# Expert layer on one core: eight blocks for the relu's output, two of four pairs rounded by ScalarE

## The chip, the cores and the metric

The kernel is one program on one core of a Trainium2 chip. Its five engines are written here as the profile writes them: PE (TensorE; PEld is its weight load), DVE (VectorE), ACT (ScalarE), POOL (GpSimd) and SP (SyncE, which issues DMAs here). Each engine works through its own list of instructions in order and is held up only by semaphores. The metric is the device time of one launch in microseconds; lower is better.

## The reference, cut to what matters

Two layers run one after the other. The change lies in the first, a mixture of experts over 16 x 256 tokens of width 256:

```python
h = h_norm * gamma[:, None, :] + beta[:, None, :]          # gamma, beta from small tables per batch
probs = softmax(h_flat @ router_w); gates, idx = top_k(probs, 2)
hid  = relu(einsum('nd,edf->nef', h_flat, exp_w1) + exp_b1)   # 8 experts, 256 -> 1024
eout = einsum('nef,efd->ned', hid, exp_w2) + exp_b2           # 1024 -> 256
y = einsum('ned,ne->nd', eout, combine); x = x + y
```

The second layer (conditioned attention with 16 heads, then a feed-forward of width 1024) reads x and is not touched. All is fp32.

## The kernel before

**Stages.** `condition_and_route` normalises and routes the tokens (up to about 170 us of the trace) and writes every token's row to DRAM, sorted by expert. Then its expert stage runs over 39 tiles (`TILES`) of 256 tokens, each with one expert. After it `transformer` runs, from about 698 us.

**Splitting.** A product of fp32 numbers is made of three products of numbers in fp32r, a shorter format: each operand is rounded (the tile with `hi` in its name) and the rest, operand minus `hi`, is the second tile (`lo`); `PASSES` takes hi x hi, hi x lo and lo x hi. So each of four things has to be split for every tile: the tokens (htokT, from the PSUM bank ps_t), four parts of w1, the relu's output (hidT, four pairs g = 0 to 3 of 128x512) and four parts of w2. Both weights of all experts are resident in SBUF.

**Work of one tile t.** PE: `up(t)`, 48 matmuls into the four banks ps_h, one bank for each pair; `turn_in(t+1)`, four transposes of the next tokens into ps_t; `down(t-1)`, 48 matmuls into ps_y, in four parts k that need hidT pair k and w2 part k. `up(t)` starts with the semaphores htokT_split and w1_split, `down(t-1)` with y_ready (the previous result has been taken out of ps_y), w2_split and the pair's hidT_even or hidT_odd.

Who splits what, in the order of each list, before the change:

- ACT (`body`, L434 on): relu of blocks 0 to 3, rounding of w1 parts 0 to 3 for tile t+1, `take_in(t+1)` (rounds the tokens out of ps_t), relu 4, relu 5, w2 part 0, relu 6, w2 part 1, relu 7, w2 parts 2 and 3.
- DVE (`body`, L753 on): the rests of w1 parts 0 to 3 (`lower_w1`, L736), the rest of the tokens (`lower_tokens`, L741), then `split_hidden` for pairs 0 to 3: a rounding copy of each (L726), and for pairs 0 and 2 also the rest (L232); last `take_out(t-1)` (L750: ps_y plus bias into SBUF, which raises y_ready).
- POOL (`body`): the rest of pair 1 (L232), of w2 parts 0 and 1 (L357), of pair 3, of w2 parts 2 and 3.
- SP: loads tokens two tiles ahead, stores the result, loads the bias row.

The relu's output goes to `hid`, which has `HID_SLOTS` = 4 blocks of 128x256 laid over the buffer columns. Pair g therefore shares its place with pair g+2, and `relu` waits at each even f until the pair that stands there has been split:

```python
wait_free(act, sem("hidT_odd" if g % 2 else "hidT_even"), 2 * t + g // 2, alone=True)
```

That is pair g-2 of the same tile for g = 2 and 3, and pair g+2 of the tile before for g = 0 and 1.

Tiles 2 to 33 run in a hardware loop of four tiles a round, the first and last ones in straight code, with the same lists.

Of the kernel before, what the change touches and what calls it, by code (L numbers as in the profile page):

```python
# [16 lines left out]
P = 128  # L17
# [94 lines left out]
def condition_and_route(nc, ctx, io, keep):  # L112
# [79 lines left out]
    y = h2  # L192
    hid = columns[:].rearrange("p i n -> p (i n)").rearrange("p (s m) -> p s m", s=HID_SLOTS)

# [22 lines left out]

    cond = cond_weights(nc, sb, w1[:, E - 1, :])

# [7 lines left out]

    def lower_pair(eng, t, g):

        rows = slice(2 * g, 2 * g + 2)  # L230
        slots = slice(2 * g % HID_SLOTS, 2 * g % HID_SLOTS + 2)
        return eng.tensor_tensor(hidT["lo"][:, rows, :], hid[:, slots, :], hidT["hi"][:, rows, :].bitcast(F32), ALU.subtract)  # L232

# [69 lines left out]
    def _(pool):  # L303
# [47 lines left out]
        def lower_hidden(t, g):  # L351
            wait_alone(pool, sem("hid_rounded"), 2 * t + g // 2 + 1)
            lower_pair(pool, t, g).then_inc(sem("hidT_odd"), 1)

# [19 lines left out]
    def _(act):  # L374
# [39 lines left out]

        def relu(t, e, f):
            if f % 2 == 0:
                g = f // 2
                wait_alone(act, sem("up_done"), F * t + f + 2)
                wait_free(act, sem("hidT_odd" if g % 2 else "hidT_even"), 2 * t + g // 2, alone=True)
            act.activation(hid[:, f % HID_SLOTS, :], ps_h[f // 2][:, (f % 2) * TOK:(f % 2 + 1) * TOK], ACT.Relu,  # L420
                           bias=b1[:, bass.ds(e, 1), f:f + 1].rearrange("p e f -> p (e f)")).then_inc(sem("hid_ready"), 1)

        def upper_w1(t, e, k):
# [10 lines left out]
        def body(tile):  # L434
            t = tile.t
            if a_tile(t):
                e = expert_of(t)
                for f in range(4):
                    relu(t, e, f)
            if a_tile(t + 1):  # L440
                ahead = expert_of(t + 1)
                for k in range(PARTS):
                    upper_w1(t + 1, ahead, k)
                take_in(t + 1)
            if a_tile(t):
                for f, pieces in ((4, ()), (5, (0,)), (6, (1,)), (7, (2, 3))):
                    relu(t, e, f)
                    for k in pieces:
                        upper_w2(t, e, k)

# [98 lines left out]
    def _(dve):  # L549
# [171 lines left out]
        def split_hidden(t, g):  # L721
            dve.wait_ge(sem("hid_ready"), F * t + 2 * (g + 1))
            wait_free(dve, sem("w2_used"), PARTS * (t - 1) + g + 1)
            rows = slice(2 * g, 2 * g + 2)
            slots = slice(2 * g % HID_SLOTS, 2 * g % HID_SLOTS + 2)
            rounded = dve.tensor_copy(hidT["hi"][:, rows, :], hid[:, slots, :])  # L726
            if g % 2:
                rounded.then_inc(sem("hid_rounded"), 1)
            else:
                rounded.then_inc(sem("hid_upper"), 1)  # L730
                dve.wait_ge(sem("hid_upper"), 2 * t + g // 2 + 1)
                lower_pair(dve, t, g).then_inc(sem("hidT_even"), 1)

# [19 lines left out]
        def body(tile):  # L753
            t = tile.t
            if a_tile(t + 1):
                e = dve.value_load(tile_tab[0:1, 0, bass.ds(t + 1, 1)], min_val=0, max_val=E - 1)
                for k in range(PARTS):
                    lower_w1(t + 1, e, k)
                lower_tokens(t + 1)
            if a_tile(t):  # L760
                for g in range(F // 2):
                    split_hidden(t, g)
            if a_tile(t - 1):
                take_out(tile.ahead(-1))
# [54 lines left out]

def cond_weights(nc, sb, room):  # L820

    def place(rows, start, width):
# [38 lines left out]
def cond_scalar(nc, act, w, vec, sem):  # L861
# [4 lines left out]
    act.wait_ge(sem("low_ready"), 1)  # L866
    act.activation(w["exp"][:], w["low"][:], ACT.Exp).then_inc(sem("soft_exp_ready"), 1)
    act.wait_ge(sem("soft_exp_ready"), 1)
    act.activation(w["log"][:], w["exp"][:], ACT.Ln, bias=1.0).then_inc(sem("soft_log_ready"), 1)
    act.wait_ge(sem("sine_ready"), 1)  # L870
# [3 lines left out]
def cond_vector(nc, dve, w, vec, ps_a, ps_b, gamma, beta, keep, sem):  # L874
# [912 lines left out]
```

## Time and profile before

| what | value |
|---|---|
| median of 3 runs (lowest, highest) | 1508.81 us (1507.02, 1511.48) |
| the profiled execution's own time | 1508.79 us |
| its span, first to last instruction | 1507.0 us |
| mean granted TensorE clock | 0.969 |
| busy over the span | PE 85%, DVE 66%, ACT 55%, POOL 42% |
| PE busy at 400 to 500 us | 94.67 us of 100 |

Busy time of PE counts each matmul to its modelled end, and successive matmuls overlap; how fast PE goes is read from the distance between the starts. Idle time in brackets names the engine whose signal ended it. The duration of a DVE or POOL instruction includes time in which it stood still after its start.

### The profile page before, as it was taken

What the parts mean: (1) busy time and instruction counts of PE and PEld (TensorE: products, weight loads), DVE (VectorE), ACT (ScalarE), POOL (GpSimd) and SP (SyncE); (2) the same over time, 40 slices, a digit from 0 to 9 for tenths busy, and PEclk for the clock granted to TensorE, in tenths of its full rate; (3) what the DMA queues carried; (4) which work ended last, traced back from release to release, by engine and by line L of the source; (5) the groups of instructions that cost most, each with busy time, mean ns of one, the idle gap of its engine ahead of it and who ended that gap; (6) DMA issues with size and microseconds to landing.
All of it is one profiled execution on the core that took longest, in us unless ns stands there. A gap on an engine that the chain in (4) does not pass through costs nothing. (4 is left out here: it accounts for less than half of the span.)

```text
span 1507.0 us, 35099 instructions
## 1 busy us (share of the span) xinstructions
PE 1286.2 (85%) x9859; PEld 1157.2 (77%) x9859; DVE 993.0 (66%) x2956; ACT 834.4 (55%) x2208; POOL 636.0 (42%) x595
## 2 busy tenths in 40 slices
PE   2666499999999999993589999999899999999996
PEld 2555399999999999993468878887788877797875
DVE  3887567667766766775557666666666765667552
ACT  2222266655656666561166666666666766666671
POOL 1677266666666666664213233323232232322211
PEclk9999999999999999997699999999999999999997
DMA  3676311111111111113666656556565666556520
GB/s 112 228 241 205 119 36 54 49 46 44 52 52 52 52 52 44 50 40 127 208 223 202 204 174 197 174 182 209 184 191 164 202 200 201 179 166 187 184 78 14
DMA packets 184810, 202.83 MB, mean 135 GB/s; under 512 B 18192, under 2 KB 172752, under 8 KB 184720
## 3 DMA queue, kind: packets, MB, share of 16 engines
q1 hardware_dynamic: 171920, 164.19, 34.8%
q10 hardware_dynamic: 6624, 20.84, 4.3%
q0 software_dynamic: 6176, 16.79, 3.3%
q8 instruction: 33, 0.54, 0.1%
q14 instruction: 57, 0.47, 0.1%
HBM read 155.89 MB, written 41.68 MB: 131 GB/s over the span
## 5 line engine op out<-in xcount | busy, mean ns | idle before, releaser
L1197 ACT ACTIVATE bias<-bias,neg_max 128x256 f32<-128x256 f32 x512 | 255.4, 501 | 207.3 <-DVE neg_max L1509 207.1
L420 ACT ACTIVATE columns<-ps_h,b_columns 128x256 f32<-128x256 f32 x312 | 134.6, 471 | 190.1 <-DVE hidT_lo L232 102.8
L357 POOL TENSOR_TENSOR w_lo<-w,w_hi 128x512 fp32r<-128x512 f32 x156 | 222.0, 1436 | 0.3
L1509 DVE CUSTOM_DVE_ANT_0 bias<-ps_s,bias 128x256 f32<-128x256 f32 x512 | 194.2, 416 | 31.5 <-PE ps_s L1285 14.9
L532 PE MATMUL ps_y<-w_hi,hidT_hi 128*128 128x256 f32 x624 | 181.3, 290 | 21.3 <-DVE token_rows L750 21.1
L519 PE MATMUL ps_h<-htokT_hi,w_hi 128*128 128x256 f32 x624 | 182.5, 293 | 11.0 <-DVE htokT_lo L741 10.4
L232 POOL TENSOR_TENSOR hidT_lo<-columns,hidT_hi 128x512 fp32r<-128x512 f32 x78 | 100.1, 1283 | 209.2 <-DVE hidT_hi L726 209.2
L736 DVE TENSOR_TENSOR w_lo<-w,w_hi 128x512 fp32r<-128x512 f32 x156 | 102.7, 715 | 119.7 <-ACT w_hi L425 119.7
L1283 PE MATMUL ps_s<-mask_f,minus_ident 128*128 128x256 f32 x512 | 155.4, 325 | 27.9 <-DVE neg_max L1509 15.4
L519 PE MATMUL ps_h<-htokT_hi,w_lo 128*128 128x256 f32 x624 | 178.5, 286 | 0.0
L519 PE MATMUL ps_h<-htokT_lo,w_hi 128*128 128x256 f32 x624 | 178.3, 286 | 0.0
L532 PE MATMUL ps_y<-w_lo,hidT_hi 128*128 128x256 f32 x624 | 177.3, 284 | 0.0
L532 PE MATMUL ps_y<-w_hi,hidT_lo 128*128 128x256 f32 x624 | 177.2, 284 | 0.0
L1297 PE MATMUL ps_p<-const,bias 128*128 128x128 f32 x1024 | 158.0, 277 | 14.5 <-ACT bias L1197 14.2
L1149 POOL TENSOR_TENSOR act_lo<-up_f,act_hi 128x512 fp32r<-128x512 f32 x64 | 82.6, 1291 | 208.2 <-ACT act_hi L1241 208.2
L726 DVE CAST hidT_hi<-columns 128x512 fp32r<-128x512 f32 x156 | 128.8, 825 | 31.6 <-ACT columns L420 29.7
L1283 PEld LDWEIGHTS ps_s<-mask_f,minus_ident 128*128 128x128 f32 x512 | 99.6, 195 | 60.5 <-DVE neg_max L1509 34.4
L532 PEld LDWEIGHTS ps_y<-w_hi,hidT_hi 128*128 128x128 f32 x624 | 120.2, 193 | 30.1 <-issue 22.6
L519 PEld LDWEIGHTS ps_h<-htokT_hi,w_hi 128*128 128x128 f32 x624 | 121.4, 195 | 18.8 <-issue 12.6
L1297 PEld LDWEIGHTS ps_p<-const,bias 128*128 128x128 f32 x1024 | 117.2, 142 | 24.0 <-issue 14.0
L1285 PE MATMUL ps_s<-k_stack,q_stack 128*128 128x256 f32 x512 | 135.3, 286 | 0.0
L1131 POOL TENSOR_TENSOR rstd<-mv,minus_half 128x2 f32<-128x2 f32 x32 | 23.1, 723 | 263.0 <-DVE mv L1568 175.2
(265 smaller groups left out, 3501.1 us busy)
## 6 DMA issues: line engine op xcount, KB each, us to landing
bias<-bias_dram SPq DMA_DIRECT2D x128, 512.0 KB, 3.8
w<-w_dram ACTq DMA_DIRECT2D x32, 512.0 KB, 4.7
xin<-dispatch SPq DMA_DIRECT2D x39, 256.0 KB, 2.7
expert_out<-token_rows SPq DMA_DIRECT2D x39, 256.0 KB, 2.2
q_stack<-q_hi_rows SPq DMA_DIRECT2D x64, 128.0 KB, 2.9
k_stack<-k_hi_rows SPq DMA_DIRECT2D x64, 128.0 KB, 2.8
q_stack<-q_lo_rows SPq DMA_DIRECT2D x64, 128.0 KB, 2.9
k_stack<-k_lo_rows SPq DMA_DIRECT2D x64, 128.0 KB, 2.9
```

Source lines behind the costliest of these rows:

```text
L232: return eng.tensor_tensor(hidT["lo"][:, rows, :], hid[:, slots, :], hidT["hi"][:, rows, :].bitcast(F32), ALU.subtract)
L357: pool.tensor_tensor(w2_part["lo"][:, k, :], w2_piece(e, k), w2_part["hi"][:, k, :].bitcast(F32), ALU.subtract).then_inc(sem("w2_split"), 1)
L420: act.activation(hid[:, f % HID_SLOTS, :], ps_h[f // 2][:, (f % 2) * TOK:(f % 2 + 1) * TOK], ACT.Relu, bias=b1[:, bass.ds(e, 1), f:f + 1]. ...
L519: last = pe.matmul(ps_h[f // 2][:, (f % 2) * TOK:(f % 2 + 1) * TOK], w1_part[a][:, C * (f // 4) + c, (f % 4) * P:(f % 4 + 1) * P], htokT[b ...
L532: last = pe.matmul(ps_y[j][:, 0:D], hidT[a][:, f, j * P:(j + 1) * P], w2_part[b][:, k, (f % 2) * D:(f % 2 + 1) * D], start=(f == 0 and n = ...
L726: rounded = dve.tensor_copy(hidT["hi"][:, rows, :], hid[:, slots, :])
L736: dve.tensor_tensor(w1_part["lo"][:, k, :], w1_piece(e, k), w1_part["hi"][:, k, :].bitcast(F32), ALU.subtract).then_inc(sem("w1_split"), 1)
L1197: act.activation(head_rows(h, j), head_rows(h, j), ACT.Exp, scale=-1.0, bias=neg_max[par][:, h, j:j + 1], accum_out=total[par][:, h, j:j + ...
L1283: pe.matmul(ps_s[h % 2][:, j * T:(j + 1) * T], minus_ident[:], mask_f[par][:, j, :], start=True, stop=False)
L1285: last = pe.matmul(ps_s[h % 2][:, j * T:(j + 1) * T], q_stack[par][:, h, j * P:(j + 1) * P].bitcast(F32R), k_stack[par][:, h // 2, :].bitc ...
L1297: last = pe.transpose(ps_p[h % 2][:, kt * T + j * P:kt * T + (j + 1) * P], head_rows(h, j)[:, kt * P:(kt + 1) * P], ident)
L1509: dve.tensor_tensor_reduce(head_rows(h, j), ps_s[h % 2][:, j * T:(j + 1) * T], head_rows(h, j), -1.0, LARGEST, ALU.add, ALU.min, neg_max[p ...
```

## The change

Three things change.

1. `hid` gets eight blocks: pairs 0 and 1 in the two halves of columns, pair 2 in the buffer xn (free in this stage), pair 3 in a new buffer hid_more. `relu` now waits only until the same pair of the tile before has been split.
2. Pairs 1 and 3 are rounded by ACT (`round_hidden`), no longer by DVE. The rests stay where they were: 0 and 2 on DVE, 1 and 3 on POOL.
3. The lists of ACT and DVE are put in another order: on both the tokens of the next tile come after w1 parts 0 and 1 instead of after all four, and on ACT all eight relus come before the tokens.

To make room for hid_more, five small tables of the conditioning (pre, neg, low, exp, log) are placed in the last expert's part of the w2 buffer, before that part is loaded.

```diff
-    hid = columns[:].rearrange("p i n -> p (i n)").rearrange("p (s m) -> p s m", s=HID_SLOTS)
+    hid = [columns[:, i, :].rearrange("p (s m) -> p s m", s=2) for i in range(2)] + [keep["xn"][:], sb("hid_more", [P, 2, TOK])[:]]
...
+            g = f // 2
             if f % 2 == 0:
-                g = f // 2
                 wait_alone(act, sem("up_done"), F * t + f + 2)
-                wait_free(act, sem("hidT_odd" if g % 2 else "hidT_even"), 2 * t + g // 2, alone=True)
+                wait_free(act, sem("hidT_odd" if g % 2 else "hidT_even"), 2 * (t - 1) + g // 2 + 1, alone=True)
...
+        def round_hidden(t, g):
+            act.wait_ge(sem("hid_ready"), F * t + 2 * (g + 1))
+            wait_free(act, sem("w2_used"), PARTS * (t - 1) + g + 1, alone=True)
+            act.activation(hidT["hi"][:, 2 * g:2 * g + 2, :], hid[g], ACT.Copy).then_inc(sem("hid_rounded"), 1)
...
             if a_tile(t + 1):
                 ahead = expert_of(t + 1)
-                for k in range(PARTS):
-                    upper_w1(t + 1, ahead, k)
+                upper_w1(t + 1, ahead, 0)
+                upper_w1(t + 1, ahead, 1)
+            if a_tile(t):
+                for f in range(4, F):
+                    relu(t, e, f)
+            if a_tile(t + 1):
                 take_in(t + 1)
+                upper_w1(t + 1, ahead, 2)
+                upper_w1(t + 1, ahead, 3)
             if a_tile(t):
-                for f, pieces in ((4, ()), (5, (0,)), (6, (1,)), (7, (2, 3))):
-                    relu(t, e, f)
-                    for k in pieces:
-                        upper_w2(t, e, k)
+                upper_w2(t, e, 0)
+                round_hidden(t, 1)
+                upper_w2(t, e, 1)
+                upper_w2(t, e, 2)
+                round_hidden(t, 3)
+                upper_w2(t, e, 3)
...
-            rounded = dve.tensor_copy(hidT["hi"][:, rows, :], hid[:, slots, :])
-            if g % 2:
-                rounded.then_inc(sem("hid_rounded"), 1)
-            else:
-                rounded.then_inc(sem("hid_upper"), 1)
-                dve.wait_ge(sem("hid_upper"), 2 * t + g // 2 + 1)
-                lower_pair(dve, t, g).then_inc(sem("hidT_even"), 1)
+            dve.tensor_copy(hidT["hi"][:, 2 * g:2 * g + 2, :], hid[g]).then_inc(sem("hid_upper"), 1)
+            dve.wait_ge(sem("hid_upper"), 2 * t + g // 2 + 1)
+            lower_pair(dve, g).then_inc(sem("hidT_even"), 1)
...
-                for k in range(PARTS):
-                    lower_w1(t + 1, e, k)
+                lower_w1(t + 1, e, 0)
+                lower_w1(t + 1, e, 1)
                 lower_tokens(t + 1)
+                lower_w1(t + 1, e, 2)
+                lower_w1(t + 1, e, 3)
             if a_tile(t):
-                for g in range(F // 2):
-                    split_hidden(t, g)
+                split_hidden(t, 0)
+                split_hidden(t, 2)
...
-        "pre": sb("pre", [P, C, B]), "neg": sb("neg", [P, C, B]), "low": sb("low", [P, C, B]),
-        "exp": sb("exp", [P, C, B]), "log": sb("log", [P, C, B]),
+        **{name: more[:, i * C * B:(i + 1) * C * B].rearrange("p (c b) -> p c b", c=C)
+           for i, name in enumerate(("pre", "neg", "low", "exp", "log"))},
```

DVE's list for the second tile, in the straight code ahead of the loop, before the change, from the tokens of the next tile on (columns is where the relu's blocks stand, token_rows the result):

```order
L736 TENSOR_TENSOR w_lo<-w,w_hi 128x512
L741 TENSOR_TENSOR htokT_lo<-ps_t,htokT_hi 128x512
L726 CAST hidT_hi<-columns 128x512
L232 TENSOR_TENSOR hidT_lo<-columns,hidT_hi 128x512
L726 CAST hidT_hi<-columns 128x512 x2
L232 TENSOR_TENSOR hidT_lo<-columns,hidT_hi 128x512
L726 CAST hidT_hi<-columns 128x512
L750 TENSOR_TENSOR token_rows<-ps_y,b_row 128x256 x2
```

And the same place in the changed kernel, from the rest of w1 part 1 on:

```order
L742 TENSOR_TENSOR w_lo<-w,w_hi 128x512
L747 TENSOR_TENSOR htokT_lo<-ps_t,htokT_hi 128x512
L742 ISA
L742 TENSOR_TENSOR w_lo<-w,w_hi 128x512
L742 ISA
L742 TENSOR_TENSOR w_lo<-w,w_hi 128x512
L736 CAST hidT_hi<-columns 128x512
L231 TENSOR_TENSOR hidT_lo<-columns,hidT_hi 128x512
L736 CAST hidT_hi<-xn 128x512
L231 TENSOR_TENSOR hidT_lo<-xn,hidT_hi 128x512
L756 TENSOR_TENSOR token_rows<-ps_y,b_row 128x256 x2
```

Two of four casts are gone between the tokens and the result, and two weight rests have moved behind the tokens.

ACT's list in the loop before the change, from the tokens to the second block of the third pair (ISA and REGISTER_ALU rows set up addresses and waits):

```order
L413 ACTIVATE htokT_hi<-ps_t 128x512 [waits up_done]
L68 REGISTER_ALU
L68 REGISTER_ALU [waits up_done]
L420 ISA [waits hidT_even]
L420 ACTIVATE columns<-ps_h,b_columns 128x256
L420 ISA
L420 ACTIVATE columns<-ps_h,b_columns 128x256
L68 ISA
L429 ISA [waits w2_used]
L429 ACTIVATE w_hi<-w 128x512
```

The changed kernel at the same place, from the tokens on:

```order
L412 ACTIVATE htokT_hi<-ps_t 128x512 [waits up_done]
L429 ISA [waits up_done]
L429 ACTIVATE w_hi<-w 128x512
L429 ISA [waits up_done]
L429 ACTIVATE w_hi<-w 128x512
L68 ISA
L433 ISA [waits w2_used]
L433 ACTIVATE w_hi<-w 128x512
L68 REGISTER_ALU [waits hid_ready]
L425 ACTIVATE hidT_hi<-columns 128x512 [waits w2_used]
```

The relus have left this place (they stand ahead of the tokens now), w1 parts 2 and 3 stand behind the tokens, and the rounding of pair 1 stands among the w2 parts, behind a wait for w2_used. PE's and POOL's lists are the same in both kernels.

## Rows read from the trace of the kernel before

**Rows 1.** Windows: stretch, its length, busy time per engine, granted clock, DMA.

```profile
400.00:500.00 100.00, 94.67 (x762) 91.42 (x761) 69.90 (x99) 60.75 (x129) 62.30 (x46) 1.00 0.17 52
```

**Rows 2.** Waits, 220 to 690 us: who for whom, total, times, longest.

```profile
POOL hidT_lo L232 <- DVE hidT_hi L726: 173.5, 72, 4.5
...
ACT columns L420 <- DVE hidT_lo L232: 94.9, 36, 2.8
...
PE ps_y L532 <- DVE token_rows L750: 20.7, 36, 3.7
...
PE ps_h L519 <- DVE htokT_lo L741: 6.5, 31, 0.2
```

**Rows 3.** Timeline of PE, one tile in the loop: start, us, what, idle before.

```profile
402.21 0.38 PE L532 MATMUL ps_y<-w_hi,hidT_hi 128*128 128x256 f32 x1 [0.48 <-DVE token_rows L750]
...
407.94 0.28 PE L532 MATMUL ps_y<-w_hi,hidT_lo 128*128 128x256 f32 x1
408.46 0.38 PE L519 MATMUL ps_h<-htokT_hi,w_hi 128*128 128x256 f32 x1 [0.24 <-DVE htokT_lo L741]
...
414.31 0.60 PE L507 MATMUL ps_t<-const,xin 128*128 128x128 f32 x4
415.40 0.38 PE L532 MATMUL ps_y<-w_hi,hidT_hi 128*128 128x256 f32 x1 [0.49 <-DVE token_rows L750]
```

**Rows 4.** Timeline of PE in the second and third tile.

```profile
192.24 0.60 PE L507 MATMUL ps_t<-const,xin 128*128 128x128 f32 x4
192.59 0.37 PE L532 MATMUL ps_y<-w_hi,hidT_hi 128*128 128x256 f32 x1
...
198.43 0.28 PE L519 MATMUL ps_h<-htokT_hi,w_hi 128*128 128x256 f32 x1
...
204.20 0.60 PE L507 MATMUL ps_t<-const,xin 128*128 128x128 f32 x4
```

**Rows 5.** Timeline of DVE, the same tile as rows 3.

```profile
404.98 2.63 DVE L736 TENSOR_TENSOR w_lo<-w,w_hi 128x512 fp32r<-128x512 f32 x4 [2.99 <-ACT w_hi L425]
407.53 0.68 DVE L741 TENSOR_TENSOR htokT_lo<-ps_t,htokT_hi 128x512 fp32r<-128x512 f32 x1
408.13 0.41 DVE L726 CAST hidT_hi<-columns 128x512 fp32r<-128x512 f32 x1
408.57 0.69 DVE L232 TENSOR_TENSOR hidT_lo<-columns,hidT_hi 128x512 fp32r<-128x512 f32 x1
...
411.37 1.67 DVE L232 TENSOR_TENSOR hidT_lo<-columns,hidT_hi 128x512 fp32r<-128x512 f32 x1
412.95 1.52 DVE L726 CAST hidT_hi<-columns 128x512 fp32r<-128x512 f32 x1
414.40 0.74 DVE L750 TENSOR_TENSOR token_rows<-ps_y,b_row 128x256 f32<-128x256 f32 x2
```

**Rows 6.** Timeline of POOL beside it, from two windows.

```profile
411.05 1.43 POOL L357 TENSOR_TENSOR w_lo<-w,w_hi 128x512 fp32r<-128x512 f32 x1
...
412.49 1.71 POOL L357 TENSOR_TENSOR w_lo<-w,w_hi 128x512 fp32r<-128x512 f32 x1
...
415.85 2.54 POOL L357 TENSOR_TENSOR w_lo<-w,w_hi 128x512 fp32r<-128x512 f32 x2
```

**Rows 7.** Timeline of ACT, the same tile.

```profile
404.13 2.20 ACT L425 ACTIVATE w_hi<-w 128x512 fp32r x4 [0.33 <-issue]
...
409.46 0.84 ACT L420 ACTIVATE columns<-ps_h,b_columns 128x256 f32<-128x256 f32 x2 [2.66 <-DVE hidT_lo L232]
410.19 0.63 ACT L429 ACTIVATE w_hi<-w 128x512 fp32r x1
```

**Rows 8.** Timeline, the last two tiles: PE, then DVE.

```profile
677.81 0.39 PE L532 MATMUL ps_y<-w_hi,hidT_hi 128*128 128x256 f32 x1 [0.85 <-DVE token_rows L750]
...
687.55 0.44 PE L532 MATMUL ps_y<-w_hi,hidT_hi 128*128 128x256 f32 x1 [3.72 <-DVE token_rows L750]
...
695.09 0.76 DVE L750 TENSOR_TENSOR token_rows<-ps_y,b_row 128x256 f32<-128x256 f32 x2 [7.59 <-PE ps_y L532]
```

More of the change, by code:

```diff
@@ L216, in condition_and_route @@
     consts_need = 16 * 2
-    cond = cond_weights(nc, sb, w1[:, E - 1, :])
+    cond = cond_weights(nc, sb, w1[:, E - 1, :], w2[:, E - 1, :])
     def w1_piece(e, k):
@@ L226, in w2_piece, with lower_pair @@
         return w2[:, bass.ds(e, 1), k * 512:(k + 1) * 512].rearrange("p e n -> p (e n)")
-    def lower_pair(eng, t, g):
+    def lower_pair(eng, g):
         rows = slice(2 * g, 2 * g + 2)
-        slots = slice(2 * g % HID_SLOTS, 2 * g % HID_SLOTS + 2)
-        return eng.tensor_tensor(hidT["lo"][:, rows, :], hid[:, slots, :], hidT["hi"][:, rows, :].bitcast(F32), ALU.subtract)
+        return eng.tensor_tensor(hidT["lo"][:, rows, :], hid[g], hidT["hi"][:, rows, :].bitcast(F32), ALU.subtract)
     block = ctx.enter_context(nc.Block())
@@ L352, in lower_hidden @@
             wait_alone(pool, sem("hid_rounded"), 2 * t + g // 2 + 1)
-            lower_pair(pool, t, g).then_inc(sem("hidT_odd"), 1)
+            lower_pair(pool, g).then_inc(sem("hidT_odd"), 1)
         def lower_w2(t, e, k):
@@ L415, in relu @@
         def relu(t, e, f):
+            g = f // 2
             if f % 2 == 0:
-                g = f // 2
                 wait_alone(act, sem("up_done"), F * t + f + 2)
-                wait_free(act, sem("hidT_odd" if g % 2 else "hidT_even"), 2 * t + g // 2, alone=True)
-            act.activation(hid[:, f % HID_SLOTS, :], ps_h[f // 2][:, (f % 2) * TOK:(f % 2 + 1) * TOK], ACT.Relu,
+                wait_free(act, sem("hidT_odd" if g % 2 else "hidT_even"), 2 * (t - 1) + g // 2 + 1, alone=True)
+            act.activation(hid[g][:, f % 2, :], ps_h[f // 2][:, (f % 2) * TOK:(f % 2 + 1) * TOK], ACT.Relu,
                            bias=b1[:, bass.ds(e, 1), f:f + 1].rearrange("p e f -> p (e f)")).then_inc(sem("hid_ready"), 1)
+        def round_hidden(t, g):
+            act.wait_ge(sem("hid_ready"), F * t + 2 * (g + 1))
+            wait_free(act, sem("w2_used"), PARTS * (t - 1) + g + 1, alone=True)
+            act.activation(hidT["hi"][:, 2 * g:2 * g + 2, :], hid[g], ACT.Copy).then_inc(sem("hid_rounded"), 1)
         def upper_w1(t, e, k):
@@ L723, in split_hidden @@
             wait_free(dve, sem("w2_used"), PARTS * (t - 1) + g + 1)
-            rows = slice(2 * g, 2 * g + 2)
-            slots = slice(2 * g % HID_SLOTS, 2 * g % HID_SLOTS + 2)
-            rounded = dve.tensor_copy(hidT["hi"][:, rows, :], hid[:, slots, :])
-            if g % 2:
-                rounded.then_inc(sem("hid_rounded"), 1)
-            else:
-                rounded.then_inc(sem("hid_upper"), 1)
-                dve.wait_ge(sem("hid_upper"), 2 * t + g // 2 + 1)
-                lower_pair(dve, t, g).then_inc(sem("hidT_even"), 1)
+            dve.tensor_copy(hidT["hi"][:, 2 * g:2 * g + 2, :], hid[g]).then_inc(sem("hid_upper"), 1)
+            dve.wait_ge(sem("hid_upper"), 2 * t + g // 2 + 1)
+            lower_pair(dve, g).then_inc(sem("hidT_even"), 1)
         def lower_w1(t, e, k):
@@ L772 @@
 UNROLL = 4
-HID_SLOTS = 4
 class Tile:
@@ L817, in pipeline, with cond_weights @@
     step(B // 2, 1, False, False, True)
-def cond_weights(nc, sb, room):
+def cond_weights(nc, sb, room, more):
     def place(rows, start, width):
@@ L866, in cond_scalar @@
     act.wait_ge(sem("low_ready"), 1)
-    act.activation(w["exp"][:], w["low"][:], ACT.Exp).then_inc(sem("soft_exp_ready"), 1)
+    act.activation(w["exp"], w["low"], ACT.Exp).then_inc(sem("soft_exp_ready"), 1)
     act.wait_ge(sem("soft_exp_ready"), 1)
-    act.activation(w["log"][:], w["exp"][:], ACT.Ln, bias=1.0).then_inc(sem("soft_log_ready"), 1)
+    act.activation(w["log"], w["exp"], ACT.Ln, bias=1.0).then_inc(sem("soft_log_ready"), 1)
     act.wait_ge(sem("sine_ready"), 1)
@@ L914, in cond_vector @@
     s.then(last)
-    s.then(dve.tensor_scalar(w["neg"][:], w["pre"][:], -1.0, None, ALU.mult))
-    dve.tensor_tensor(w["low"][:], w["pre"][:], w["neg"][:], ALU.min).then_inc(sem("low_ready"), 1)
+    s.then(dve.tensor_scalar(w["neg"], w["pre"], -1.0, None, ALU.mult))
+    dve.tensor_tensor(w["low"], w["pre"], w["neg"], ALU.min).then_inc(sem("low_ready"), 1)
     dve.wait_ge(sem("soft_log_ready"), 1)
-    s.then(dve.scalar_tensor_tensor(gamma[:], w["pre"][:], 0.0, w["log"][:], ALU.max, ALU.add))
+    s.then(dve.scalar_tensor_tensor(gamma[:], w["pre"], 0.0, w["log"], ALU.max, ALU.add))
     s.then(dve.tensor_scalar(gamma[:], gamma[:], 1e-8, None, ALU.add))
```

## The prediction

> **What bounds the kernel now.** I read the page first. PE is busiest, and the slices show a long even stretch from about 200 to 690 us: the expert stage, nearly a third of the launch and the only part whose lists change. The window in its middle has PE busy for 94.67 of 100 us at a granted clock of 1.00 [rows 1]. That looks like a stage that only fewer matmuls could shorten. It isn't quite: busy time runs to each matmul's modelled end, so the next view is PE's timeline, and there the starts count. In one tile of the loop `down` starts at 402.21, `up` at 408.46, the transposes at 414.31, the next `down` at 415.40 [rows 3]. The period is 13.19 us. `down` takes 5.85 (its 48th start at 407.94, one more step of 0.12), then 0.40 passes until `up`; `up` takes 5.85; from the transposes to `down` is 1.09. The rows name who ended the two gaps: DVE with the rest of the tokens, and DVE with the taking out of ps_y.
>
> How short these gaps can be is seen at the second tile, where nothing is waited for: transposes to `down` 0.35 (192.24 to 192.59), `down` to `up` 5.84 with no gap (to 198.43), `up` to the next transposes 5.77 (204.20) [rows 4]. So PE by itself needs 5.84 + 5.77 + 0.35 = 11.96 us for a tile. Each loop tile carries about 1.2 us that isn't PE's.
>
> Third, the view of waits over the stage, for what stands behind DVE: POOL waits 173.5 us for DVE's rounding copies, ACT's relu 94.9 us for a DVE rest, and PE, by comparison, only 20.7 and 6.5 us [rows 2]. A ring runs through ACT, DVE and POOL: the third pair's relu waits until the first pair is split, since both use one place. In the timelines: DVE ends that rest at 409.26 (408.57 + 0.69) [rows 5], the relu starts at 409.46, after 2.66 us of idling [rows 7]. DVE's later casts and POOL's pieces follow from it, and PE is served late at both joints. The ring, not PE, sets 13.1.
>
> **How DVE and POOL share time.** DVE's cast takes 0.41 us at 408.13 but 1.52 at 412.95; its rest takes 0.69 at 408.57 and 1.67 at 411.37 [rows 5]. POOL has a w2 piece from 411.05 and one from 412.49, of 1.43 and 1.71, against 2.54 for two undisturbed (1.27 each) [rows 6]. The ends fit a lock held by one at a time: the rest ends at 413.04, 0.54 after POOL's first piece ended (412.49), the cast at 414.47, 0.27 after the second (414.20); and that second ends 1.16 after DVE's rest. So I take as exclusive 0.54 us for a DVE rest, 0.28 for a cast, 1.16 for a POOL piece. The token rest and the taking out read PSUM; I let them run freely.
>
> The Trainium skill (SBUF — State Buffer, "Who interferes with whom") says that a DVE instruction with two SBUF inputs contends with a GpSimd instruction that reads SBUF, and that the port pair is held exclusively. By that rule, the trace agrees with its 1.67 against 0.69; what it would do to this change is the second rival below.
>
> **The change, part by part.** I lay one tile on PE's clock, `up(t)` starting at 0 and the next at 11.96, and walk each list with the distances of the rows: ACT 0.37 for a relu (two from 409.46, next start 410.19), 0.53 for a weight or hidden copy, 0.5 for the tokens; semaphore to next engine about 0.2 (409.26 to 409.46) [rows 7]. PE's pairs end at 1.6, 3.0, 4.5, 5.9, the transposes at 6.4, the parts of `down(t-1)` at 7.7, 9.2, 10.7, 12.1 (48 starts in four parts of 1.46, plus 0.28).
>
> *Eight blocks.* The relu now waits only for the same pair one tile back, split long before (below). Removed: 2.66 us of ACT idling in each tile. ACT: relus 0 to 3 end by 4.1 (held by PE's pairs), w1 parts 0 and 1 by 5.3, relus 4 to 7 by 7.0, tokens by 7.5, w1 parts 2 and 3 by 8.5.
>
> *Two roundings on ACT.* ACT gets 2 x 0.53 = 1.05 us, DVE loses two casts. Behind w2_used ACT does w2 part 0 (8.4 to 9.0), pair 1 (waits for 9.2, ends 10.0), w2 parts 1 and 2 (by 11.5), pair 3 (waits for 12.1, ends 12.9), w2 part 3 by 13.5. That is an added wait with a whole list queued behind it; the next relus need their pair at 11.96 + 1.8 = 13.8, so it holds back nothing. ACT works 8 x 0.37 + 8 x 0.53 + 0.5 + 1.05 = 8.8 us of 11.96, plus about 0.3 for reading the expert's number.
>
> *Tokens before w1 parts 2 and 3.* DVE: w1 part 0 at 5.0, parts 0 and 1 done by 7.7 with POOL in between, token rest by 8.4. `up(t+1)` needs it at 11.96 with 0.25 of signal: 3.3 us of slack where there was -0.4. Then w1 parts 2 and 3 by 9.6 (needed at 14.8), pair 0 by 10.6, the cast of pair 2 at 10.9 to 12.1 behind POOL, its rest by 13.8 behind POOL, the taking out of `down(t-1)` by 14.5. `down(t)` starts at 18.1: 3.4 us of slack where there was -0.5.
>
> *POOL.* Pair 1 from 10.2 to 11.8, w2 parts 0 and 1 by 13.2 and 15.0, pair 3 by 16.2, w2 parts 2 and 3 by 17.5 and 19.2; needed by PE from 18.1 in steps of 1.46, so the tightest, w2 part 2, has 3.5 us. The lock's demand is 6 x 1.16 + 6 x 0.54 + 2 x 0.28 = 10.8 of 11.96 us.
>
> The same walk with the old lists, with the waits for shared places, comes back to 13.15 per tile, which is what the rows have; that is why I trust it.
>
> *The small tables* in the w2 buffer: the same instructions on the same shapes in a stage long before; cost 0. No wait is added, since that part of w2 is loaded near the end of routing. SP's loads come as before, two tiles ahead: 0.
>
> So PE becomes the bound in the loop. **The sum.** From `down(0)` at 192.59 to `down(37)` at 677.81 there are 37 periods, 485.2 us, mean 13.11 [rows 4, 8]. At 11.96 each: 442.5, or 42.7 less. The loop's joints have never run without a wait in this trace, and PE's own queue may need something at them. By the second tile it needs 0; by a loop tile at most the whole gap, 0.40 + 0.74 = 1.14. I take 0.04 a tile, near the former, since the join of `up` to `down` there was seamless: 12.0, so 41.2 less.
>
> *The end.* Before, `down(38)` started at 687.55, 9.74 after `down(37)`, since DVE took ps_y out late, and the last taking out began at 695.09, 17.3 after 677.81 [rows 8]. Now: pair 2's rest stands behind POOL until 7.3, taking out ends at 8.0, `down(38)` starts at 8.3 and its last part, whose weights POOL delivers at 12.2, ends at 14.2: 14.5 instead of 17.3, 2.8 less. PE's gap of 5.84 to 8.3 can still cost a while at half clock, as that of 3.72 did before (0.12 a matmul became 0.21 for some fifteen of them, 1.4 us); I take 2.2. The start is unchanged: until 192.24 the first tiles are held by DMA, tokens and relus that come in the same order; 0.
>
> Sum: 1508.8 - 41.2 - 2.2 = 1465.4, say 1465. The profiled execution's 1508.79 equals the median of 1508.81, so the sum needs no shift.
>
> A page speaks against moving the roundings. The Trainium skill (Perfetto Trace Analysis, "Optimizing Scalar/DVE Operations") says of work that either engine can do: "If a DVE performance mode (2x or 4x) is available, it will be faster". The rows agree for an undisturbed cast, 0.41 against ACT's 0.63; beside POOL they have 1.52. By the rule two casts on ACT lose 0.2 us each, and the stage would gain only from the blocks and the order.
>
> **The rivals.**
>
> *PE's own queue becomes the bound.* Each joint has several semaphores against registers, and a loop round ends every four tiles. If each tile pays 0.45 beyond 11.96, saved are 37 x 0.70 = 26 + 2: 1481. Against it: the seamless joint at 198.43, which is already the loop's first. Chance 0.11.
>
> *The shared port holds DVE.* Demand is 10.8 of 11.96, and chance decides who meets whom. If all six POOL pieces block DVE in full, DVE's tile is 6 x 0.61 + 2 x 0.44 + 0.6 + 0.74 = 5.9 of work + 6 x 1.16 = 12.8, period 12.8: saved 37 x 0.27 + 1 = 11, 1498; half of the way there, 1482. For it: of the four DVE instructions on the hidden pairs in the rows two were blocked [rows 5]. Against it: the slack of 3.3 us at both joints. Chance 0.08. The port rule of the skill is this rival's mechanism.
>
> *Slower: the port and the added waits together.* The same 12.8, and DVE also idles for ACT's w1 copies (2.5 us in the walk), because ACT now sits behind w2_used waits that follow PE. From 0.3 us of idling a tile that can't be filled, the period passes 13.11. With 0.9 it is 13.7: 37 x 0.6 = 22 more, 1531. Chance 0.04.
>
> *No change.* The ring is closed elsewhere, by one I haven't seen, at 13.1: 1508. Chance 0.03.
>
> **How the numbers follow.** The forecast has 0.74, with its own range 1460 (11.96 and the whole 2.8, rounded down) to 1472 (12.2 a tile). The range reaches over the queue's rival and half of the port's: 1460 to 1484. A measurement of this kernel tells about 0.3% (4.5 us) from no change: faster 0.93, same 0.03, slower 0.04.
>
> **What would show it.** In PE's timeline: transposes to `down` 0.35 and `down` to `up` 0.12 without an idle in brackets, period 12.0. In the waits: PE for token_rows and htokT_lo gone but for the edges, ACT's relu waiting for PE and no longer for hidT_lo, POOL's idling moved to ACT's hidT_hi. DVE's taking out should start some 2 us after `up` starts, not 6. If PE still idles at a joint, the named releaser decides: DVE means the port, "issue" means the queue. Wrong altogether if the period stays at 13.

## The result and the profile after

The changed kernel takes 1461.01 us (1458.6 to 1463.81), the kernel before 1508.76 on the same chip: ratio 0.9683, 95% interval 0.9656 to 0.9710. The forecast was 1465, range 1460 to 1484. The profiled execution took 1463.81 us with a span of 1462.0, against 1507.0.

The window in the middle of the expert stage (stretch, length, busy time of PE, PEld, DVE, ACT, POOL, granted clock, DMA), which answers to [rows 1]:

```profile
400.00:500.00 100.00, 100.00 (x839) 100.00 (x838) 87.87 (x94) 78.60 (x162) 75.94 (x50) 1.00 0.17 53
```

PE goes from 94.67 to 100.00. Its share of busy time rose by only five points, yet it issued 839 matmuls in place of 762, a tenth more: the starts count, not the busy time. DVE has fewer instructions (94 for 99) and is busier, 87.87 us for 69.90.

The waits from 220 to 650 us (who for whom, total, times, longest), in answer to [rows 2], with the rows that matter here:

```profile
POOL hidT_lo L231 <- ACT hidT_hi L425: 99.9, 36, 5.2
DVE w_lo L742 <- ACT w_hi L429: 52.0, 19, 5.0
ACT columns L419 <- PE ps_h L531: 43.1, 59, 2.8
ACT hidT_hi L425 <- PE ps_y L544: 29.7, 53, 0.8
...
ACT columns L419 <- DVE hidT_lo L231: 4.4, 5, 1.9
PE ps_y L544 <- DVE token_rows L756: 2.8, 2, 1.9
```

ACT's wait for DVE's rest of the relu fell from 94.9 to 4.4 us; ACT is now paced by PE. PE's wait for token_rows fell from 20.7 us in 36 tiles to 2.8 in two, and its wait for htokT_lo is gone.

PE's timeline at a loop tile, in answer to [rows 3, 4] (start, duration, what):

```profile
402.31 0.28 PE L544 MATMUL ps_y<-w_hi,hidT_lo 128*128 128x256 f32 x1
402.43 0.28 PE L531 MATMUL ps_h<-htokT_hi,w_hi 128*128 128x256 f32 x1
...
408.19 0.60 PE L519 MATMUL ps_t<-const,xin 128*128 128x128 f32 x4
408.55 0.36 PE L544 MATMUL ps_y<-w_hi,hidT_hi 128*128 128x256 f32 x1
...
420.14 0.60 PE L519 MATMUL ps_t<-const,xin 128*128 128x128 f32 x4
```

`down` to `up` is one step of 0.12, transposes to `down` 0.36, the period 420.14 - 408.19 = 11.95. From one `down` to the next, all but one of the loop's periods are 11.94 to 11.96. The one exception is 13.02, looked at below.

DVE over one tile, in answer to [rows 5]:

```profile
407.31 0.74 DVE L756 TENSOR_TENSOR token_rows<-ps_y,b_row 128x256 f32<-128x256 f32 x2
407.97 2.82 DVE L742 TENSOR_TENSOR w_lo<-w,w_hi 128x512 fp32r<-128x512 f32 x2
410.71 0.68 DVE L747 TENSOR_TENSOR htokT_lo<-ps_t,htokT_hi 128x512 fp32r<-128x512 f32 x1
411.32 1.79 DVE L742 TENSOR_TENSOR w_lo<-w,w_hi 128x512 fp32r<-128x512 f32 x2
413.03 1.51 DVE L736 CAST hidT_hi<-columns 128x512 fp32r<-128x512 f32 x1
414.58 1.67 DVE L231 TENSOR_TENSOR hidT_lo<-columns,hidT_hi 128x512 fp32r<-128x512 f32 x1
416.17 1.52 DVE L736 CAST hidT_hi<-xn 128x512 fp32r<-128x512 f32 x1
417.72 1.66 DVE L231 TENSOR_TENSOR hidT_lo<-xn,hidT_hi 128x512 fp32r<-128x512 f32 x1
419.31 0.74 DVE L756 TENSOR_TENSOR token_rows<-ps_y,b_row 128x256 f32<-128x256 f32 x2
```

No brackets: DVE never idles here. At least six of its eight instructions on SBUF stand behind a POOL piece (1.5 to 1.7 us in place of 0.4 to 0.7; of the pairs of weight rests 2.82 and 1.79 in place of 1.3). The opening says that an engine is held up only by its semaphores; these rows, like [rows 5 and 6], are the exception. Its tile takes 12.00 us, against PE's 11.95. The taking out ends at 408.05 and `down` starts at 408.55, with 0.25 us to spare beyond the signal's own 0.25. PE is the bound by a hair.

Where it crossed, the same view shows the tile of 13.02 us (PE's row first, then DVE's, then POOL's):

```profile
277.12 0.38 PE L544 MATMUL ps_y<-w_hi,hidT_hi 128*128 128x256 f32 x1 [0.83 <-DVE token_rows L756]
...
263.66 2.82 DVE L742 TENSOR_TENSOR w_lo<-w,w_hi 128x512 fp32r<-128x512 f32 x2
...
267.01 2.93 DVE L742 TENSOR_TENSOR w_lo<-w,w_hi 128x512 fp32r<-128x512 f32 x2
...
276.14 0.74 DVE L756 TENSOR_TENSOR token_rows<-ps_y,b_row 128x256 f32<-128x256 f32 x2
276.81 1.69 DVE L742 TENSOR_TENSOR w_lo<-w,w_hi 128x512 fp32r<-128x512 f32 x2
...
274.19 3.15 POOL L356 TENSOR_TENSOR w_lo<-w,w_hi 128x512 fp32r<-128x512 f32 x2
```

Both pairs of weight rests take over twice their 1.3 us there, and the four instructions on the hidden pairs, not shown, take 1.52 to 1.67 each, so all eight were slowed beside POOL. DVE's tile took 276.81 - 263.66 = 13.15 us, and PE lost 1.08. In a second profiled run of the same kernel no tile was disturbed. Which phase POOL and DVE fall into is not the same in every run.

The end, in answer to [rows 8] (PE, then DVE):

```profile
643.02 0.39 PE L544 MATMUL ps_y<-w_hi,hidT_hi 128*128 128x256 f32 x1 [1.93 <-DVE token_rows L756]
...
650.56 0.76 DVE L756 TENSOR_TENSOR token_rows<-ps_y,b_row 128x256 f32<-128x256 f32 x2 [7.60 <-PE ps_y L544]
```

The books, from the two profiled executions: from `down(0)` (192.59, now 192.42) to `down(37)` (677.81, now 635.17) 485.2 became 442.75, 42.5 less; from there to the last taking out 17.28 became 15.39, 1.9 less; what comes before the first and after the last of these is 0.17 and 0.47 us shorter. 42.5 + 1.9 + 0.6 is the span's 45.0.

### The profile page after: what moved, and what is told of

It is laid out like the page before. It is cut to its first block and busy times, and to the rows that moved or that the text cites. A ratio compares the mean times of both kernels' runs of the same rounds, so it can differ in the third digit from the quotient of the medians.

```text
span 1462.0 us, 35033 instructions
## 1 busy us (share of the span) xinstructions
PE 1266.3 (87%) x9859; PEld 1153.8 (79%) x9859; DVE 1021.6 (70%) x2878; ACT 884.4 (60%) x2286; POOL 674.3 (46%) x595
## 5 line engine op out<-in xcount | busy, mean ns | idle before, releaser
L356 POOL TENSOR_TENSOR w_lo<-w,w_hi 128x512 fp32r<-128x512 f32 x156 | 244.5, 1588 | 0.0
L1516 DVE CUSTOM_DVE_ANT_0 bias<-ps_s,bias 128x256 f32<-128x256 f32 x512 | 194.3, 417 | 30.1 <-PE ps_s L1292 13.1
L742 DVE TENSOR_TENSOR w_lo<-w,w_hi 128x512 fp32r<-128x512 f32 x156 | 151.6, 1011 | 59.8 <-ACT w_hi L429 58.8
L531 PE MATMUL ps_h<-htokT_hi,w_hi 128*128 128x256 f32 x624 | 178.6, 286 | 3.2 <-DVE htokT_lo L747 3.2
L1304 PE MATMUL ps_p<-const,bias 128*128 128x128 f32 x1024 | 158.8, 278 | 14.4 <-ACT bias L1204 14.1
L531 PEld LDWEIGHTS ps_h<-htokT_lo,w_hi 128*128 128x128 f32 x624 | 121.6, 195 | 0.0
L531 PEld LDWEIGHTS ps_h<-htokT_hi,w_lo 128*128 128x128 f32 x624 | 121.6, 195 | 0.0
L544 PEld LDWEIGHTS ps_y<-w_lo,hidT_hi 128*128 128x128 f32 x624 | 120.3, 193 | 0.0
```

Of the source, the lines that this page charges most:

```text
L356: pool.tensor_tensor(w2_part["lo"][:, k, :], w2_piece(e, k), w2_part["hi"][:, k, :].bitcast(F32), ALU.subtract).then_inc(sem("w2_split"), 1)
L531: last = pe.matmul(ps_h[f // 2][:, (f % 2) * TOK:(f % 2 + 1) * TOK], w1_part[a][:, C * (f // 4) + c, (f % 4) * P:(f % 4 + 1) * P], htokT[b ...
L544: last = pe.matmul(ps_y[j][:, 0:D], hidT[a][:, f, j * P:(j + 1) * P], w2_part[b][:, k, (f % 2) * D:(f % 2 + 1) * D], start=(f == 0 and n = ...
L742: dve.tensor_tensor(w1_part["lo"][:, k, :], w1_piece(e, k), w1_part["hi"][:, k, :].bitcast(F32), ALU.subtract).then_inc(sem("w1_split"), 1)
L1304: last = pe.transpose(ps_p[h % 2][:, kt * T + j * P:kt * T + (j + 1) * P], head_rows(h, j)[:, kt * P:(kt + 1) * P], ident)
L1516: dve.tensor_tensor_reduce(head_rows(h, j), ps_s[h % 2][:, j * T:(j + 1) * T], head_rows(h, j), -1.0, LARGEST, ALU.add, ALU.min, neg_max[p ...
```

## The experiments

Each was run beside the kernel before on its own chip; there the kernel before took 1515.6 to 1517.9 us, so ratios are compared, and periods from the profiles. "Period" is the distance from `up` to `up` in the loop. The periods are the finer measure: outside the expert stage one execution differs from another by up to 16 us, whatever the kernel (from the last taking out to the end of the span: 811.4 us in the changed kernel, 827.7 in one of those below).

| kernel | ratio to before (95%) | period |
|---|---|---|
| before | 1 | 13.15 |
| the change | 0.9683 (0.9656 to 0.9710) | 11.95, once 13.02 |
| the change, again | 0.9690 (0.9663 to 0.9716) | 11.95 |
| eight blocks alone | 0.9750 (0.9717 to 0.9784) | 12.30 |
| ACT's roundings alone | 1.0315 (1.0298 to 1.0332) | 14.1, every fourth 16.2 to 16.7 |
| order of the tokens alone | 0.9990 (0.9973 to 1.0008) | 13.16 |
| blocks and order | 0.9676 (0.9641 to 0.9711) | 11.95 |
| blocks and roundings | 0.9704 (0.9664 to 0.9744) | 11.95 |
| the change, one POOL piece more | 0.9814 (0.9775 to 0.9854) | 11.95 to 13.1, mean 12.3 |
| blocks and order, one POOL piece more | 0.9959 (0.9933 to 0.9986) | 12.92 |
| blocks and roundings, another end | 0.9692 (0.9661 to 0.9724) | 11.95 |

**The parts alone.** In all of these `hid`, the lists and who rounds are set one by one from the two kernels; the short diffs are against the kernel named.

Eight blocks alone, against the changed kernel (ACT's list goes back likewise, relus 6 and 7 between the w2 parts too):

```diff
-                lower_w1(t + 1, e, 0)
-                lower_w1(t + 1, e, 1)
-                lower_tokens(t + 1)
-                lower_w1(t + 1, e, 2)
-                lower_w1(t + 1, e, 3)
+                for k in range(PARTS):
+                    lower_w1(t + 1, e, k)
+                lower_tokens(t + 1)
...
-                split_hidden(t, 0)
-                split_hidden(t, 2)
+                for g in range(F // 2):
+                    split_hidden(t, g)
```

> The changed kernel with eight blocks alone: DVE rounds all four pairs, and both lists stand in the old order. Theory of the shared place (the relu of the third pair waiting for the first pair's split closed the ring): nearly the whole gain is here, a period of 12.0 to 12.3 us and a time of 1461 to 1475 us; ACT's waits for hidT_lo are gone. Rival of DVE's load (the casts on DVE beside POOL set the pace, and their going to ACT gave the gain): less than half of the gain, a period of 12.6 or more, 1487 us or more.

Ratio 0.975, period 12.30, and some 79% of the gain (2.5 of 3.17 per cent; 74% by the mean distance of the `down`s, 13.11 to 12.26 to 11.97). "Nearly the whole gain" was a little too much, less than half was far off. No wait of ACT for hidT_lo is left. The shared place was what closed the ring. What stops it at 12.30 is DVE. Its window, then its rows in one tile and POOL's beside them:

```profile
400.00:500.00 100.00, 100.00 (x816) 97.98 (x815) 99.45 (x106) 67.78 (x138) 78.42 (x50) 1.00 0.18 55
```

```profile
399.54 6.19 DVE L738 TENSOR_TENSOR w_lo<-w,w_hi 128x512 fp32r<-128x512 f32 x4
405.66 0.68 DVE L743 TENSOR_TENSOR htokT_lo<-ps_t,htokT_hi 128x512 fp32r<-128x512 f32 x1
...
400.03 1.74 POOL L231 TENSOR_TENSOR hidT_lo<-hid_more,hidT_hi 128x512 fp32r<-128x512 f32 x1
401.73 3.45 POOL L356 TENSOR_TENSOR w_lo<-w,w_hi 128x512 fp32r<-128x512 f32 x2
```

DVE is busy 99.45 of 100 us. Four weight rests, 2.5 us undisturbed, take 6.19: they meet POOL's last three pieces of the tile before.

The roundings alone, four blocks kept:

```diff
+    hid = [columns[:, i, :].rearrange("p (s m) -> p s m", s=2) for i in range(2)] * 2
...
+                relu(t, e, 4)
+                relu(t, e, 5)
+                upper_w2(t, e, 0)
+                round_hidden(t, 1)
+                relu(t, e, 6)
+                upper_w2(t, e, 1)
+                relu(t, e, 7)
+                upper_w2(t, e, 2)
+                round_hidden(t, 3)
+                upper_w2(t, e, 3)
```

> The roundings of pairs 1 and 3 on ACT alone: four blocks, old order otherwise (the rounding of pair 1 stands before relu 6, as it must, since relu 6 needs its place; that of pair 3 after w2 part 2). Shared place: no gain, and since the rounding waits for w2_used in the middle of the relus it may close a longer ring, a period of 13.1 to 14.1 us, 1508 to 1545 us. Rival of DVE's load: DVE is relieved, a period of 12.6 or less, 1490 us or less.

Slower by 3.15%: the direction and the period of the ring (14.1) were as the shared place wants them. The time, 1565 us, is beyond its range, since every fourth tile takes 2.0 to 2.6 us more; by the periods that is 16 of the 48 us lost. ACT's rows show the chain and that tile:

```profile
314.68 0.84 ACT L419 ACTIVATE columns<-ps_h,b_columns 128x256 f32<-128x256 f32 x2 [2.94 <-DVE hidT_lo L231]
...
318.22 0.47 ACT L419 ACTIVATE columns<-ps_h,b_columns 128x256 f32<-128x256 f32 x1 [1.66 <-POOL hidT_lo L231]
...
323.59 0.84 ACT L419 ACTIVATE columns<-ps_h,b_columns 128x256 f32<-128x256 f32 x2 [2.45 <-issue]
```

ACT waits for DVE, rounds pair 1, then waits for POOL's rest of it before relu 6: its own rounding has become a link of the ring. The link isn't the one expected: the rounding itself waits for nothing, since the view has no wait of ACT for w2_used; what costs is POOL's rest behind it. The 2.45 us of "issue" stand where the loop turns over. DVE has two casts fewer, and with the ring still closed the kernel gains nothing by it.

The order of the tokens alone, on the kernel before. The other half of the new order, all relus ahead of the tokens, can't be had with four blocks: relu 4 would wait for the split of pair 0, which stands on DVE behind the tokens that ACT rounds only after it.

```diff
-                for k in range(PARTS):
-                    upper_w1(t + 1, ahead, k)
+                upper_w1(t + 1, ahead, 0)
+                upper_w1(t + 1, ahead, 1)
                 take_in(t + 1)
+                upper_w1(t + 1, ahead, 2)
+                upper_w1(t + 1, ahead, 3)
```

> The kernel before with the tokens ahead of w1 parts 2 and 3 on ACT and DVE, nothing else. Shared place: the ring is as long as before, 13.1 us, 1506 to 1510 us. Rival of the order (the late token rest is what PE waits for, so serving it two instructions earlier gives the gain): PE's wait for htokT_lo goes and the time falls by 10 to 20 us.

No difference (0.9990). PE's wait for htokT_lo does go, with the token rest ready 1.05 us before `up` where it had been 0.25; the period stays 13.16. A wait named in the profile was removed and nothing was gained: ACT's wait for DVE's rest before relu 4 is as it was (87.0 us in 33 tiles, 86.8 before, 220 to 650 us), so the ring is as long.

Eight blocks and the new order, all roundings on DVE:

```diff
-                round_hidden(t, 1)
...
-                round_hidden(t, 3)
...
-                split_hidden(t, 0)
-                split_hidden(t, 2)
+                for g in range(F // 2):
+                    split_hidden(t, g)
```

> The changed kernel with all four roundings on DVE (eight blocks and new order kept). Shared place: PE stays the bound, 11.95 to 12.2 us, 1461 to 1470 us; the port is asked for 11.3 of 11.95 us, so more tiles than one may be held by DVE. Rival of DVE's load: a clear loss against the changed kernel, period 12.4 or more, 1478 us or more.

0.9676, the same as the change within the intervals, and the same period. So with blocks and order, the roundings on ACT are worth nothing that can be measured. The slack of the taking out before `down` is 1.2 to 3.1 us in every tile, where the changed kernel has tiles with 0.24. DVE's casts of pairs 0 to 2 run undisturbed here (rows of one tile: DVE, then POOL):

```profile
410.12 0.41 DVE L734 CAST hidT_hi<-columns 128x512 fp32r<-128x512 f32 x1
410.57 0.69 DVE L231 TENSOR_TENSOR hidT_lo<-columns,hidT_hi 128x512 fp32r<-128x512 f32 x1
411.18 0.42 DVE L734 CAST hidT_hi<-columns 128x512 fp32r<-128x512 f32 x1
411.51 0.42 DVE L734 CAST hidT_hi<-xn 128x512 fp32r<-128x512 f32 x1
...
411.75 1.34 POOL L231 TENSOR_TENSOR hidT_lo<-columns,hidT_hi 128x512 fp32r<-128x512 f32 x1 [2.70 <-DVE hidT_hi L734]
```

POOL can't start before DVE has rounded pair 1, so the rest and all three casts have started ahead of it. The fourth cast, at 413.56, has 1.51 us.

Blocks and roundings with the old order of the tokens. It differs from the eight blocks alone in two things: the roundings on ACT, and relus 6 and 7, which stand ahead of the w2 parts here and between them there:

```diff
-                upper_w1(t + 1, ahead, 0)
-                upper_w1(t + 1, ahead, 1)
+                for k in range(PARTS):
+                    upper_w1(t + 1, ahead, k)
+                take_in(t + 1)
...
-            if a_tile(t + 1):
-                take_in(t + 1)
-                upper_w1(t + 1, ahead, 2)
-                upper_w1(t + 1, ahead, 3)
```

> The changed kernel (eight blocks, two roundings on ACT) with the old order: w1 parts 0 to 3, tokens, then relus 4 to 7. Theory that only blocks and order matter: the order is what the eight blocks lack, so this is like eight blocks alone, a period of about 12.3 us with DVE never idle, ratio to the kernel before 0.972 to 0.978. Rival, that the roundings on ACT give DVE room: 11.95 us, ratio 0.966 to 0.970, since DVE has 0.9 us less to do than with the blocks alone.

11.95 in every tile, with the token rest 1.35 us or more ahead of `up`. Against 12.30 for the blocks alone this is the rival's result. DVE was busy for 397.7 us of 220 to 620 us there and is for 320.8 here, so most likely it is the roundings on ACT that give it room; that the place of relus 6 and 7 has no part in it is not shown. The two ratios (0.9704 and 0.9750) have overlapping intervals, so the difference rests on the periods. Taken with the run before: once the eight blocks are there, either the new order or this list with the roundings on ACT brings the period to PE's own, and having both adds nothing.

**How near the port is.** One more POOL piece a tile, on the changed kernel; no other engine waits for it, but the last piece of POOL's list comes later by it:

```diff
+                wait_alone(pool, sem("w2_upper"), PARTS * t + 4)
+                pool.tensor_tensor(w2_part["lo"][:, 3, :], w2_piece(e, 3), w2_part["hi"][:, 3, :].bitcast(F32), ALU.subtract).then_inc(sem("twice"), 1)
+                wait_alone(pool, sem("twice"), t + 1)
                 lower_w2(t, e, 3)
```

> The changed kernel with one more POOL piece a tile: the rest of w2 part 3 is made twice, the second after the first (nothing else waits for the first). If the port is nearly full (10.8 of 11.95 us held, 12.0 with this), the period becomes 12.3 to 13 us and PE's waits for DVE or POOL come back, ratio 0.975 to 0.99. Rival, the port has room because its holdings overlap in part: 11.95 us still, ratio 0.966 to 0.970.

1.3% slower than the change by the ratios. Periods run 11.95, 12.5, 12.0, 13.1 and over again, mean 12.3; PE waits for token_rows again. POOL's own list isn't full: of 220 to 620 us it is busy for 355.8, and it waits 41.2 us for ACT's roundings from 220 to 650 us; DVE is busy for 386.5 of the 400. So the port has no room for one piece of 1.27 us.

> The extra POOL piece again, now on eight blocks and new order with all roundings on DVE. By the sum of holdings (11.3 + 1.2 = 12.5) this must be slower than the same piece on the changed kernel: 12.6 to 13 us, ratio 0.98 to 0.99. Rival, from the even slack of this kernel without the piece (2 to 3 us in every tile, where the changed kernel has tiles with 0.3): when DVE rounds, POOL is released by DVE itself and meets it less often, so the loss is not larger than on the changed kernel.

Ratio 0.9959, 12.92 in every tile: almost the whole gain is gone. The period is in the range of the sum of holdings, the ratio is beyond its 0.98 to 0.99, and the rival from the even slack fell. But the mechanism isn't the sum's: PE waits here for POOL's w2 rests (22.3 us in 31 tiles, 220 to 620 us), while DVE's taking out ends 1.6 us before `down` in every tile and POOL waits 65.1 us for DVE's rounding of pair 1. So the even slack of the kernel without the extra piece was DVE's; the scarce thing is the length of POOL's list from that rounding on. This is read from the waits; no run separates it from the port.

**How far the rest stands behind PE.** 32 instead of 48 matmuls in `up`; the pass left out is the one of the weights' rests with the rounded tokens (the expectation names the wrong operands), so the result is less exact:

```diff
-                    for n, (a, b) in enumerate(PASSES):
+                    for n, (a, b) in enumerate(PASSES[:2]):
```

> The changed kernel with 32 instead of 48 matmuls in up: the third pass (rounded weights are not multiplied with the tokens' rests or the like) is left out, 1.9 us of PE a tile. If PE alone were the bound with the rest far behind: a period of 10.0 us, some 70 us less. If the port stands close behind PE, as 10.8 us of holdings say: 11.0 to 11.7 us, 10 to 35 us less than the changed kernel, with PE waiting for DVE again.

1469.74 us in a single run, 0.9685 of the kernel before on its chip, where the changed kernel has 0.9683. That looks like no gain, but it is one execution, and the part that nothing was changed in took long: 827.7 us from the last taking out to the end, for 811.4 in the changed kernel. The expert stage, from the first start of `up` to the last taking out, took 466.6 us (173.76 to 640.32), against 476.3 in the changed kernel (174.26 to 650.56) and 473.9 in the second run of it. So leaving out a third of `up` saved 7 to 10 us of the stage, where PE alone would have given some 70:

```profile
640.32 0.76 DVE L756 TENSOR_TENSOR token_rows<-ps_y,b_row 128x256 f32<-128x256 f32 x2 [6.19 <-PE ps_y L544]
```

The period is 10.03 in every few tiles and 10.9 to 14.5 in between, mean 11.8. The window has DVE at 90.74:

```profile
400.00:500.00 100.00, 88.45 (x717) 86.83 (x717) 90.74 (x95) 78.71 (x165) 80.01 (x53) 0.98 0.18 56
```

PE's waits are for token_rows (42.3 us in 26 tiles, 220 to 620 us) and for DVE's rests of the hidden pairs. That is a little worse than the 11.0 to 11.7 and the 10 to 35 us expected.

The same on the old order:

> The third pass of up left out (32 instead of 48 matmuls in up), now with the old order of the tokens. If what held the former run at 11.8 us a tile is the ring through DVE and the port whatever the order: 11.5 to 12.3 us and again no gain over the changed kernel. If it was the new order, in which ACT releases DVE and POOL at once: clearly less, 11.0 us or below, and DVE not near full.

1445.42 us in a single run, 0.954 of the kernel before, mean period 11.4, DVE at 92.56 of 100 us. Its stage took 450.5 us (174.33 to 624.86), 23 to 26 less than with all matmuls:

```profile
624.86 0.76 DVE L752 TENSOR_TENSOR token_rows<-ps_y,b_row 128x256 f32<-128x256 f32 x2 [6.20 <-PE ps_y L540]
```

Neither expectation holds in full: there is a gain over the changed kernel, and with PE out of the way the old order is the better one, by 0.4 us a tile, but the waits for DVE (token_rows, 35.2 us in 29 tiles, and the rests of the hidden pairs) hold it far above 10.03 too. Why the old order is the better one here was not tried.

**A version that might beat the change.** The change again, and beside it blocks and roundings with the old order, where DVE takes ps_y out ahead of pair 2's split in the last tile:

```diff
             if a_tile(t):
                 split_hidden(t, 0)
-                split_hidden(t, 2)
+                if not last_tile:
+                    split_hidden(t, 2)
             if a_tile(t - 1):
                 take_out(tile.ahead(-1))
+            if last_tile:
+                split_hidden(t, 2)
```

> The changed kernel once more, on the same chip as the next one, for a narrower interval: ratio 0.966 to 0.971 by every theory.

> Eight blocks and two roundings on ACT with the old order (which had 11.95 us in every tile), and in the last tile DVE takes ps_y out ahead of pair 2's split. Theory that what is left above PE's own 11.95 us is one disturbed tile (1.1 us) and the late taking out at the end (about 0.7 us): 1.5 to 2 us less than the changed kernel, 0.1%, which the interval can't separate from it; PE's wait for token_rows before the last down goes from 1.9 to about 1.2 us. Rival, that the order of the tokens matters by itself: slower than the changed kernel by more than 3 us.

0.9690 and 0.9692 (0.9661 to 0.9724): not told apart. PE's wait for token_rows before the last `down` fell from 1.9 to 0.8 us, and 0.9 us of waiting for a POOL rest came in its place. No version here beats the change by more than can be measured.

## Why the prediction was right

- *PE's own period, 11.96, and the joints.* Right: 11.95, with `down` to `up` 0.12 and transposes to `down` 0.36. The 0.04 us a tile set aside for PE's queue was not needed. 42.5 us saved over the 37 periods, where 41.2 were forecast.
- *The lower end of the range.* 1460 was "rounded down" from 11.96 and the whole 2.8, which give 1508.8 - 42.7 - 2.8 = 1463.3. The median, 1461.0, is below that sum; only the rounding put it inside.
- *The ring through the shared place.* Right, and now shown: the eight blocks alone bring 12.30, the roundings alone a loss, and as much of the new order as four blocks allow nothing.
- *Two roundings on ACT.* The forecast priced them at 1.05 us on ACT, hidden, and put no price on what they bring. Beside the new order they bring nothing (0.9676 without, 0.9683 with); beside the old order of the tokens most likely the 0.35 us a tile. Put on four blocks they cost 3%. The forecast quotes half a sentence of the Trainium skill (Perfetto Trace Analysis, "Optimizing Scalar/DVE Operations") as speaking against the move; the sentence goes on: "but if DVE is saturated, offloading some work to Scalar (or even GPSIMD) may make sense". The runs agree with both halves: the cast stays at 0.41 on DVE where POOL is still held back and the move brings nothing, and where DVE was busy for 99.45 of 100 us the kernel with the move has the shorter period.
- *The slack at the joints.* The step that was off. The walk had 3.3 us before `up` and 3.4 before `down`, beyond the signal's 0.25; measured in the loop, with the signal in them, are 1.4 to 3.8 and 0.24 to 3.7, so the narrowest tiles had nothing left before `down`. DVE's taking out was to start some 2 us after `up`; it starts 1.7 to 5.0 after it, in the disturbed tile 6.2. The walk let DVE meet POOL in about four of eight instructions; the rows of one tile have six or more, and once all eight. For each tile DVE was busy for 10.2 us instead of 9.3 (340.0 and 283.4 of 220 to 620 us, over the periods), with two casts fewer. The rival of the shared port (0.08) came true in one period of 37, for 1.1 us; the run with one more POOL piece shows that it was at most 1.3 us of POOL's time a tile away. That PE stayed the bound in nearly every tile is thus in part luck: the slack on which the forecast rested its 0.08 wasn't there.
- *Smaller readings.* "Of the four DVE instructions on the hidden pairs in the rows two were blocked": the trace has six in that tile, and a third, the cast at 410.33, took 1.00 in place of 0.41. The walk calls w2 part 2 the tightest on POOL with 3.5 us; by its own steps part 3 has 3.3 (19.2 for 22.5). The walk with the old lists, from which the forecast drew its trust, isn't laid out and can't be followed.
- *The slower rival.* It needed DVE idle for ACT behind its w2_used waits. That idling is there, 52 us in 19 tiles (before it was 99.1 in 33, both from 220 to 650 us), but in tiles in which DVE is early.
- *The end.* 1.9 us against 2.2. `down(38)` started 7.85 after `down(37)` (8.3 in the forecast), and then ran slower, as the forecast feared: the granted clock is 0.50 from 643.7 to 646.7 us, with 0.21 from start to start, and 1.00 from 647 us on, with 0.12. From the start of `down(38)` to the last taking out both kernels have 7.54.
- *The sum.* 1465 against 1461.0. The profiled execution has 1463.8, 1.6 below the sum: 1.3 more in the periods, 0.6 before and after the stage that the forecast put at nothing, 0.3 less at the end. The other 2.8 us are the spread of the runs.

## What to carry to other kernels

When the busiest engine looks near full, read the distance between its starts with and without a wait in front: here 95% busy hid 1.2 us in 13.15. When every engine waits for another, look for a place in memory that two stages of the same work share; giving the second its own place can be worth more than shortening any member of the ring, and moving work between engines before that can make the ring longer. Then ask how far the next bound is: here it lay a fraction of a microsecond behind, and a third fewer matmuls in one product bought 7 to 10 us of the stage in one order of the lists and 23 to 26 in another, of some 70. And when a single run seems to show no gain, look at the stage that was changed by itself: the rest of the launch can hide it.

## What the runs showed of the hardware

A DVE instruction that stands behind POOL counts as busy: a cast has 0.41 us alone and 1.52 beside POOL. So DVE's busy time rose from 9.3 to 10.2 us a tile while it had two instructions fewer. The instructions of DVE that read PSUM kept their times beside POOL, from 220 to 620 us of every kernel: the token rest 0.67 to 0.69, the two of the taking out 0.74 or 0.75. And in the kernel with the roundings alone ACT stood still for 2.35 to 2.85 us with nothing to wait for that the profile shows, once in four tiles, where the loop turns over; in the other kernels no such wait of ACT from 220 to 620 us is longer than 0.57. What it is was not tried.
